# Quantized codes turned by DMA in a fused perceiver block: pairs 0 to 12, with the clip and the integer product one place later in the round

## The reference, cut to what matters

```
x = x + cross_attention(layernorm(x), ctx)     # 16 heads, latent width 32
x = x + self_attention(layernorm(x))           # one head of width 128, then Wo and a bias
x = x + ffn(layernorm(x))
```

```
xh    = layernorm(x) @ hadamard                                  # 512 x 512
scale = clip(max(abs(xh), axis=-1), 1e-5) / 7
xq    = clip(round(xh / scale), -8, 7) * scale                   # 4-bit codes, one scale per row
wq    = ternary(weight) * wscale                                 # -1, 0, 1 times one scale per output row
out   = xq @ wq.T
```

## Time and profile before

| | |
|---|---|
| time, median of 3 runs | 319.33 us (318.48 to 320.63) |
| the profiled execution | 318.31 us, of which the span of the trace is 316.5 us |
| mean granted TensorE clock | 0.997 |
| busy | TensorE 96%, VectorE 78%, ScalarE 66%, GpSimd 28% |
| DMA traffic | 25.2 MB in the span, 80 GB/s |

### The profile page before, as it was taken

One profiled execution on the slowest core, in us unless ns is written; L12 is line 12 of the kernel. 1 busy time (PEld: TensorE's weight loads), 2 busy tenths in 40 slices (PEclk: granted clock), 3 DMA queues, 4 the chain that ended last, 5 costly groups with the idle time before them and its releaser, 6 DMA issues.

```text
span 316.5 us, 8395 instructions
## 1 busy us (share of the span) xinstructions
PE 303.5 (96%) x3110; PEld 210.6 (67%) x3110; DVE 247.6 (78%) x530; ACT 208.3 (66%) x587; POOL 89.6 (28%) x129
## 2 busy tenths in 40 slices
PE   8996899999999999999999999999999999998993
PEld 6864767667576867667576866667586867656642
DVE  1489979986879778887879778887979778896266
ACT  1387687767695877767595877767685777783300
POOL 2006504240323224240323224240323224242311
PEclk9999999999999999999999999999999999999998
DMA  7992202050401403050302303050302001000001
GB/s 227 356 363 88 101 5 97 2 201 0 136 4 65 136 11 124 0 197 2 133 0 70 129 5 127 0 188 10 133 2 68 2 21 48 2 34 2 33 0 66
DMA packets 13480, 25.23 MB, mean 80 GB/s; under 512 B 3216, under 2 KB 3984, under 8 KB 13456
## 3 DMA queue, kind: packets, MB, share of 16 engines
q1 hardware_dynamic: 13456, 24.91, 23.1%
HBM read 20.71 MB, written 4.19 MB: 79 GB/s over the span
## 4 chain that ended last, share of the span: by engine, by line
PE 78%; DVE 11%; ACT 7%; issue 2%; POOL 1%; DVEq 0%; POOLq 0%
PE ps L983 10%; PE ps L1037 9%; PE ps L934 6%; PE ps L1103 5%; ACT prob L368 4%; PE ps L1083 4%; PE ps L1041 4%; PE ps L1158 3%; PE ps L1129 3%; PE ps L1135 3%; PE ps L944 3%; PE ps L1010 2%; DVE mx L596 2%; PE ps L994 2%; PE ps L972 2%
## 5 line engine op out<-in xcount | busy, mean ns | idle before, releaser
L368 ACT ACTIVATE prob<-ps,nmx,qk_scale 128x128 f32<-128x128 f32 x240 | 90.1, 470 | 34.2 <-DVE nmx L600 34.1
L983 PE MATMUL ps<-had_s,x3t 128*128 128x512 f32 x104 | 48.0, 604 | 0.4 <-ACT x3t L362 0.4
L596 DVE TENSOR_REDUCE mx<-ps 128x8 f32<-128x1024 f32 x31 | 37.8, 1219 | 11.0 <-PE ps L1103 10.8
L317 POOL TENSOR_TENSOR qk_scale<-aux,power 128x1 f32<-128x1 f32 x16 | 8.8, 550 | 98.9 <-DVE aux L618 98.9
L605 DVE TENSOR_REDUCE sum_a<-prob 128x8 f32<-128x1024 f32 x30 | 35.8, 1210 | 0.5 <-ACT prob L368 0.5
L362 ACT ACTIVATE prob_t<-ps 128x512 f32<-128x512 f32 x63 | 34.9, 624 | 0.8 <-PE ps L934 0.4
L983 PEld LDWEIGHTS ps<-had_s,x3t 128*128 128x128 f32 x104 | 18.7, 189 | 24.7 <-issue 22.8
L934 PE MATMUL ps<-ident,prob 128*128 128x128 f32 x240 | 31.6, 274 | 2.9 <-ACT prob L368 2.9
L934 PEld LDWEIGHTS ps<-ident,prob 128*128 128x128 f32 x240 | 26.8, 141 | 5.4 <-ACT prob L368 4.3
L1037 PE MATMUL ps<-x2t,wqkv_s 128*128 128x128 f32 x224 | 28.6, 281 | 0.4
L1037 PEld LDWEIGHTS ps<-x2t,wqkv_s 128*128 128x128 f32 x224 | 26.1, 191 | 2.1 <-ACT x2t L362 1.4
(11 more groups left out here) (201 smaller groups left out, 590.6 us busy)
## 6 DMA issues: line engine op xcount, KB each, us to landing
ct<-ctx_cols SPq DMA_DIRECT2D x16, 512.0 KB, 4.8
xt<-x_cols SPq DMA_DIRECT2D x16, 256.0 KB, 2.8
xr<-x_rows SPq DMA_DIRECT2D x16, 256.0 KB, 4.1
y<-res SPq DMA_DIRECT2D x15, 256.0 KB, 2.0
had_s<-hadamard SPq DMA_DIRECT2D x1, 1024.0 KB, 7.7
w_rows<-weight SPq DMA_DIRECT2D x1, 1024.0 KB, 9.9
wqkv_s<-wqkv SPq DMA_DIRECT2D x1, 768.0 KB, 9.1
wqk<-w_qk SPq DMA_DIRECT2D x2, 128.0 KB, 4.1
```

What stands on the lines that cost most here:

```text
L368: last = nc.scalar.activation(prob[:, h, :], ps[:, h // 4, (h % 4) * P:(h % 4) * P + P], ACT.Exp, bias=nmx[:, h:h + 1], scale=qk_scale[:])
L596: V.tensor_reduce(mx[:, h], ps[:, 2 * half:2 * half + 2, :].rearrange("p r (c k) -> p (r c) k", c=EC), AX.X, ALU.max).then_inc(done["mx"], 1)
L983: mm = pe.matmul(ps[:, B4, :], x3t[:, c, :], had_s[:, c, :], start=(c == 0), stop=(c == EC - 1))
```

## The change

For pairs 0 to 12 the codes are no longer turned by TensorE. SP issues four DMAs that transpose qi block by block into a new SBUF tensor, codes. SP waits for the codes (`done["qi"]`) and for the previous clip ahead of its load of xr, and issues the four DMAs behind that load. VectorE clips from codes instead of from PSUM, and does so behind the first maximum of the new scores instead of ahead of the row statistics. The order of the last steps is exchanged on both engines: TensorE does Wo ahead of the integer product, VectorE x3 ahead of prod. In the tail, where pairs 13 to 15 are still turned on TensorE, only the counts in the waits change.

```diff
+        codes = sb("codes", [P, EC, P], BF16)
...
-        qit_bank = ps[:, B4, :].bitcast(BF16)[:, 0:E]
...
+        codes_turned = sem("codes_turned")
...
+            def codes_by_dma(pair):
+                for c in range(EC):
+                    sp.dma_start(codes[:, c, :], qi[:, c * P:(c + 1) * P], transpose=True).then_inc(codes_turned, 16)
...
                     load_context(i + 3, 1 - par)
+                if quant and (not pre or i < PAIRS - 1):
+                    after(sp, done["qi"], i - 2)
+                    after(sp, read["qit"], i - 3)
                 if not pre or 1 <= i < PAIRS - 1:
                     load_rows(i + 1, 1 - par)
+                if quant and (not pre or i < PAIRS - 1):
+                    codes_by_dma(i - 2)
...
(VectorE)
-                if quant:
-                    after(dve, made["qit"], i - 2)
-                    V.tensor_scalar(qi_t[:], qit_bank.rearrange("p (c t) -> p c t", c=EC), QMIN, None, ALU.max)\
-                        .then_inc(read["qit"], 1)
                 if front and not (first and 0 <= i <= 1):
                     row_variance()
                     row_scale()
...
                     largest(i + 1, 0)
                 if quant:
+                    after(dve, codes_turned, i - 2, 16 * EC)
+                    after(dve, made["int"], i - 3)
+                    V.tensor_scalar(qi_t[:], codes[:], QMIN, None, ALU.max)\
+                        .then_inc(read["qit"], 1)
+                if self_:
+                    after(dve, made["wo"], i - 1)
...
+                    V.scalar_tensor_tensor(x3[:, 1 - par], ps[:, B3, :], rsum2[:], x2b[:], ALU.mult, ALU.add)\
+                        .then_inc(read["wo"], 1)
+                if quant:
                     after(dve, made["int"], i - 2)
...
                     V.scalar_tensor_tensor(prod[:], ps[:, B4, :], qscale[:], scale_row[:], ALU.mult, ALU.mult)\
                         .then_inc(read["int"], 1)
-                if self_:
-                    after(dve, made["wo"], i - 1)
...
(TensorE)
-                if quant:
-                    after(pe, done["qi"], i - 2)
-                    for c in range(EC):
-                        mm = pe.transpose(qit_bank[:, c * P:(c + 1) * P], qi[:, c * P:(c + 1) * P], ident_b[:])
-                    mm.then_inc(made["qit"], 1)
...
+                if self_:
+                    after(pe, read["o2t"], i - 1)
+                    pe.matmul(ps[:, B3, :], o2t[:], wo_s[:], start=True, stop=True).then_inc(made["wo"], 1)
                 if quant:
                     after(pe, read["qit"], i - 2)
                     for c in range(EC):
...
-                if self_:
-                    after(pe, read["o2t"], i - 1)
-                    pe.matmul(ps[:, B3, :], o2t[:], wo_s[:], start=True, stop=True).then_inc(made["wo"], 1)
```

More of the change, by code:

```diff
@@ L741, in body @@
                 if quant:
+                    after(dve, codes_turned, i - 2, 16 * EC)
[4 more added lines that the diff above has]
+                    after(dve, made["wo"], i - 1)
+                    after(dve, done["rsum2"], i - 1)
+                    after(dve, done["x2b"], i - 1)
+                    after(dve, done["res"], i - 3)
+                    V.scalar_tensor_tensor(x3[:, 1 - par], ps[:, B3, :], rsum2[:], x2b[:], ALU.mult, ALU.add)\
+                        .then_inc(read["wo"], 1)
+                if quant:
                     after(dve, made["int"], i - 2)
@@ L800, in quantized @@
                 after(dve, read["had"], n)
-                after(dve, made["qit"], n - 1)
+                if n > N - 2:
+                    after(dve, made["qit"], n - N + 1)
                 V.tensor_scalar(qi[:], z[:], ROUND, QMAX, ALU.subtract, ALU.min).then_inc(done["qi"], 1)
             def clipped(n, bank):
-                after(dve, made["qit"], n)
+                after(dve, made["qit"], n - N + 2)
                 after(dve, made["int"], n - 1)
```

## The result

The changed kernel takes 331.49 us (median of 4 runs, 330.28 to 332.16) beside 319.31 us for the one before; the ratio is 1.036 (95% interval 1.032 to 1.040). The forecast was 325, so the direction was right and the loss more than twice what the sum gave. The profiled span is 329.3 us against 316.5.

What follows compares the result with a forecast made beforehand. TensorE, busy 96% of the span, was taken as the bound. Per round 0.67 us added less 0.24 saved gave +0.43, in 13 rounds +5.6 us: 323.9 or 324.9, forecast 325 us, range 321 to 340.

Steps and rivals of the forecast that it cites:

- the one on the DMA transposes: SP's queue: four DMAs issued 0.53 us apart land 4.2 us after the codes, hidden; upper bound 8.6 us.
- rival 1: Codes land late on SP's queue: 17 us more, 342, at the upper bound; 333 at the middle; chance 0.28.
- the sign named for it: Integer product's wait goes back to a DMA through the clip, and even rounds are longer than odd ones.
- rival 2: SP itself is held by each transpose, 2.28 us each: 58 us in all, 383; chance 0.09.
- Added: 0.67 us x 13.: Round's end, o2t to next attended values: integer product waits for the clip, 2.94 instead of 2.27 us; 8.7 us in all.
- alone it would remain: Wo's wait of 0.32 us for ScalarE's copy of o2t, taken as hidden under the integer product's wait for the clip.
- no small VectorE operation here is under about 0.15: Lower bound for the clip's time on VectorE; bounds 0.15 and 0.43 us, 0.41 taken.
- All shift with TensorE and add nothing: VectorE's x3, prod and next round's xm, queued behind the clip, and TensorE's next write of prod's bank: no added time.
- the removed transposes: Four instructions leave TensorE each round: 0.24 us x 13 rounds, 3.1 us saved.
- the clip's old place: VectorE ahead of the row statistics: it cost 0.41 us there but held up nobody, so its removal earns nothing.
- the load of the rows: SP's load of xr behind the codes lands at 164.2 us, in time by 0.4 in the even round; cost zero.
- the traffic: The transposes' 128 KB a round are little beside the 1 MB and more already moved.

Runs made afterwards that it cites:

- one DMA: Changed kernel with one transposing DMA of 128x512 per round in place of four of 128x128; 324.32 us, ratio 1.014 against the kernel before.
- the clip ahead: Changed kernel with one 128x512 transposing DMA per round and VectorE's clip ahead of the first maximum, Wo still ahead of the integer product; 324.69 us, 1.016.
- the sum out of the way: Changed kernel with GpSimd's sum of prod and x3 (res) moved into the next round, behind x2n; 330.79 us, 1.033.
- the old order: Changed kernel with one 128x512 transposing DMA, integer product ahead of Wo, prod ahead of x3, clip ahead of the first maximum; 317.74 us, 0.992.
- GpSimd's sum later and the old order on TensorE: Changed kernel with one 128x512 DMA, integer product ahead of Wo, clip before first maximum, x3 still ahead of prod, GpSimd's sum behind next round's x2n; 320.48 us.
- a fifth DMA: Changed kernel with one more transposing DMA per round, of one block into a spare tile, ahead of the four; 344.05 us, 1.075.

## Why the prediction was wrong, step by step

**The step that failed** is the one on the DMA transposes: "I take the lower, since the queue shows overlapping transfers". It priced them at nothing, from issues 0.53 us apart. They are 1.15 to 1.28 us apart, the last of four starts 3.7 us after the first and lands 2.3 us later, and the codes come 6.6 us after the end of old line 708 in round 8, where 6.2 were to be had. One DMA in place of four gives back 7.2 us. The outcome is that of rival 1, which had 0.28: late codes in even rounds alone, and the sign named for it, a product that waits for a DMA through the clip. Its middle, 333, is near the measured 331.5. The mechanism is that of rival 2, which had 0.09: SP is held by each transpose, though for 1.23 us and not for 2.28. The overlap of two ordinary transfers on that queue was no evidence for another kind of instruction. The Trainium skill's 1.309 us for a 128x128 transpose by DMA ("VectorE: DVE Perf Modes", section "The three transpose paths") was the nearer figure for four in a row, and the trace is close to it (1.15 to 1.28 us apart). With its 0.390 us for TensorE the trace does not agree: the four blocks together took 0.40 us there. The single DMA of 128x512 shows, though, that this is a price per instruction: four blocks in one take 1.20.

The lateness is 0.45 us in rounds 6 to 10 and 0.9 to 2.0 in rounds 2, 4, 12 and 14 (changed less one DMA in the table). In round 4 the four issues took 6.17 us instead of 4.93, all of it in the last one, which landed 3.6 us after its start. In round 14 they took 4.92 as in the loop, but the last landed 3.7 us after its start instead of 2.3. Why issue or landing takes longer there is open.

**"Added: 0.67 us x 13."** The stretch grew by 0.50, since the clip takes 0.29 us and not 0.41. The Trainium skill's rule of four elements a cycle ("VectorE: DVE Perf Modes", section "Rules for kernel authors") gave an estimate of 0.28, and the trace agrees. But the sum laid the weight in the wrong place: the product does not wait for the clip for more than 0.09 us, and the wait of 0.32 for ScalarE's copy is the larger part (0.31, shown by the clip ahead). The prediction had said of it that "alone it would remain", and nearly so it came. And two terms were missing. Behind the bf16 product the next round's first two groups take 0.17 us less (0.89 and 0.53 instead of 1.01 and 0.59), and the group that followed the transposes takes 0.04 more (0.63 instead of 0.59). In odd rounds the balance is 0.50 - 0.17 - 0.23 + 0.04 = +0.14 us, as measured, against a forecast of 0.43. The bound "no small VectorE operation here is under about 0.15" was also misread: line 734 takes 0.10. Little hung on it.

**"All shift with TensorE and add nothing"** failed in even rounds. prod is later, so GpSimd's sum is later, and it meets VectorE's x2, which goes from 0.69 to 0.88 us. Another 0.17 us is lost because x2n's chain hangs on the end of the attended values, which did not come nearer with the shorter groups: xm starts 1.09 us after the round's start in both kernels. That makes the 0.37 us between 3.56 and 3.93, and with the sum out of the way 0.17 of it stayed (3.73). The even round's balance without late codes is 0.14 + 0.37 = 0.51, measured 0.50. I had looked at who waits for prod on TensorE, not at what its reader GpSimd would run beside.

**Overlooked:** in round 1 the scale row's transposes stood ahead of Wo and now stand behind it. ScalarE's copy of them starts 1.95 us after its copy of o2t instead of 0.93, and its exponentials and x3t wait behind it. So the Hadamard product of round 2 starts 2.03 us after the latents' group instead of 0.99, and the old order gives this back (0.99). The rows of ScalarE in the changed kernel:

```profile
42.82 0.30 ACT L372 ACTIVATE o2t<-ps 128x128 f32<-128x128 f32 x1
...
44.77 0.60 ACT L372 ACTIVATE scale_row<-ps 128x512 f32<-128x512 f32 x1 [1.51 <-PE ps L919]
45.39 2.20 ACT L378 ACTIVATE prob<-ps,nmx,qk_scale 128x128 f32<-128x128 f32 x6
47.47 0.68 ACT L372 ACTIVATE x3t<-ps 128x256 f32<-128x256 f32 x2
```

By an accident of these errors the order's part was nearly the forecast sum: 324.3 us with the codes in time, against 325. **Right** were: the removed transposes (0.2 us a round in the old order, 0.24 in the sum), nothing from the clip's old place, nothing from the load of the rows, nothing from the traffic, and that no gain was to be had in this order.

The rounds add up: 4.9 + 0.8 us for the order, of which 0.9 for the scale row in round 2 (1.39 against 0.50 in the loop), and 6.7 for the late codes are 12.4 of the 12.8 us between the two spans. The 0.4 left are the start and the tail.

## What to carry to other kernels

Price a new kind of DMA by its issue, not by the queue's ordinary issues: until a row shows it, the case that it holds the queue is the likelier one, and the first thing to try is one instruction for all blocks. Before moving an operation, list not only who waits for its result but what each reader will then run beside, and what its copy had been covering. The exchange of two short steps on VectorE alone cost 5.6 us here (323.4 against 317.7), and the removal of the transposes, beside which it stood, earns 1.9 (319.6 to 317.7). When rounds grow longer and nothing in them waits longer, look at the granted clock of each round.

## What the runs showed of the hardware that was not expected

- A transposing DMA holds SP's queue for 1.10 to 1.23 us in most rounds, whether it moves 32 KB (128x128 bf16) or 128 KB (128x512, 1.20 us); the longest issue of the changed kernel took 2.47. The DMA of 128x512 lands 2.9 us after its start (median; 2.6 to 4.5), the last of the four in round 8 2.3 us after its own. With GpSimd's sum later and the old order on TensorE (320.48 us) the median landing was 4.1 and the longest 5.9; why is open.
- VectorE's sum of two fp32 tiles in SBUF (128x512) goes from 0.69 us to 0.88, 1.10, 1.12 and 1.35 as GpSimd's sum of the same size overlaps it longer. In the two pairs of rows shown above it ends 0.55 and 0.56 us after GpSimd's sum has ended (161.54 after 160.99, 156.48 after 155.92), so what it loses is the overlap less 0.14 us. VectorE's operation that reads one tile from PSUM (xm, 0.69 us) ran beside the same GpSimd sum without a loss.
- After 1.64 us of standing still in the run with a fifth DMA (end of round 10), TensorE's next groups ran at the lower level of the granted clock (0.51 between 222 and 224 us). After 1.9 us in the changed kernel (end of round 4) they did not (1.00).
